# Layer 1 attention in a two-layer decoder: biases folded into the scores and the residual, values of two tokens made ahead of the outputs, weighted products between value moves

## What is computed

```
src = x                                  # (s=4, b=512, f=256): it attends over the FIRST axis, 4 long
qkv = einsum('sbf,pf->sbp', src, in_proj_weight) + in_proj_bias      # p = 3 * 1024
q, k, v = split(qkv, 3)                  # 16 heads of 64
attn = softmax(q / 8 @ k.T)              # 4 x 4 for each b and head
out = attn @ v                           # 4 x 1024 for each b
x = layernorm(x + out @ out_proj_weight.T + out_proj_bias)
```

## Time and profile before

| | |
|---|---|
| median of three runs | 2261.79 us |
| profiled execution, first to last instruction | 2256.1 us |
| busy over the span: PE / DVE / ACT / GpSimd | 89% / 68% / 51% / 42% |
| mean granted TensorE clock | 0.955 of full speed (2.4 GHz) |
| layer 1's attention in the span | from about 527 to 889 us |

### The profile page before, as it was taken

How to read it: one execution, slowest core, us unless ns; L and a number is a source line. 1 busy time by engine, 2 the same in 40 slices (tenths; PEclk the granted TensorE clock), 3 DMA queues, 4 the chain that set the end, 5 groups by cost and what they waited for, 6 DMA issues and landing times. The chain is left out here.

```text
span 2256.1 us, 35858 instructions
## 1 busy us (share of the span) xinstructions
PE 2013.2 (89%) x12740; PEld 1400.3 (62%) x12740; DVE 1528.9 (68%) x2458; ACT 1150.2 (51%) x2210; POOL 950.5 (42%) x738
## 2 busy tenths in 40 slices
PE   7898867997988985899999999999999997699997
PEld 4565547994344444556666666665666664599996
DVE  5777764555888796688788778887787886322223
ACT  3332311111457546678775877677776773233333
POOL 2233232322222131366666756575665665222223
PEclk9999988998999997999999999999999998799998
DMA  4100017211000001000000010000000001621113
GB/s 158 39 23 22 23 48 281 97 67 66 1 0 1 0 30 67 1 1 1 30 1 1 10 30 1 1 10 1 1 1 1 10 1 40 243 109 36 39 36 124
DMA packets 36714, 93.29 MB, mean 41 GB/s; under 512 B 5415, under 2 KB 24379, under 8 KB 31934
## 3 DMA queue, kind: packets, MB, share of 16 engines
q1 hardware_dynamic: 30462, 74.72, 9.2%
q0 software_dynamic: 6080, 16.29, 2.2%
HBM read 76.56 MB, written 14.44 MB: 40 GB/s over the span
## 5 line engine op out<-in xcount | busy, mean ns | idle before, releaser
L2169 POOL TENSOR_TENSOR x_total<-x_total,x_pt 128x1024 f32<-128x1024 f32 x189 | 446.4, 2362 | 172.6 <-ACT x_pt L2255 155.3
L2277 ACT ACTIVATE x_pt<-PS,x_maskf 128x512 f32<-128x512 f32 x544 | 332.1, 689 | 165.8 <-PE PS L2591 164.9
L2376 DVE TENSOR_TENSOR PS<-x_pt,PS 128x512 f32<-128x512 f32 x480 | 333.4, 695 | 65.5 <-ACT x_pt L2277 28.3
L2394 DVE TENSOR_TENSOR x_pt<-x_pt,PS 128x1024 f32<-128x1024 f32 x320 | 320.1, 1050 | 0.7 <-PE PS L2609 0.7
L2591 PE MATMUL PS<-x_qs,x_ks 64*128 64x256 f32 x2176 | 281.3, 395 | 1.5 <-ACT x_pt L2277 1.5
L2568 PE MATMUL PS<-x_pt,x_vs 128*64 128x256 f32 x2108 | 264.2, 390 | 20.5 <-ACT x_pt L2255 10.6
L2255 ACT ACTIVATE x_pt<-x_pt 128x1536 f32<-128x1536 f32 (+1 forms) x160 | 266.5, 1667 | 13.8 <-DVE x_pt L2394 13.8
L1165 PEld LDWEIGHTS PS<-m_xT,m_own 128*128 128x128 f32 x1984 | 235.4, 195 | 8.3 <-DVE m_own L1245 2.9
L1165 PE MATMUL PS<-m_xT,m_own 128*128 128x128 f32 x1984 | 236.3, 278 | 4.1 <-DVE m_own L1245 2.4
L2591 PEld LDWEIGHTS PS<-x_qs,x_ks 64*128 64x128 f32 x2176 | 199.2, 188 | 65.2 <-issue 39.3
L2568 PEld LDWEIGHTS PS<-x_pt,x_vs 128*64 128x64 f32 x2108 | 142.3, 137 | 138.5 <-issue 65.1
(11 more groups left out here) (315 smaller groups left out, 2894.3 us busy)
## 6 DMA issues: line engine op xcount, KB each, us to landing
f_w<-in_L_ffn_w SPq DMA_DIRECT2D x32, 1024.0 KB
a_ctxT<-in_ctxT SPq DMA_DIRECT2D x8, 800.5 KB, 4.4
l_w<-in_ctx SPq DMA_DIRECT2D x4, 1024.0 KB
f_w<-ys SPq DMA_DIRECT2D x16, 256.0 KB, 5.5
l_w<-in_L_attn_w SPq DMA_DIRECT2D x6, 512.0 KB
a_xT<-in_xT SPq DMA_DIRECT2D x4, 512.0 KB, 5.9
X<-in_x SPq DMA_DIRECT2D x1, 2048.0 KB, 10.9
xr<-a_xn SPq DMA_DIRECT2D x16, 128.0 KB, 1.7
```

The source lines that it names most:

```text
L2169: ins = nc.gpsimd.tensor_tensor(total2[:], first, tile[:, 2 * k + 2:2 * k + 4, :], ALU.add)
L2277: nc.scalar.activation(pt[:, s % 2, t, :].rearrange("p (h n) -> p h n", h=2), PS[:, first:first + 2, half], ACT.Identity, bias=maskf[:, b ...
L2376: ins = nc.vector.tensor_tensor(acc, tile, acc, ALU.max)
L2394: nc.vector.tensor_tensor(p_, p_, PS[:, MB, None, :].to_broadcast([P, at.stop - at.start, SPAN]), ALU.subtract).then_inc(lowered, 1)
```

## The change

The bias of a chunk is no longer added on PE. Because a softmax over keys is unchanged by terms that depend on the query alone, and the rest is linear, the query and key biases turn into one term for each query token, head and key token, made from x by a small matmul: per group, use QK (now a use of its own) multiplies the turned x by `wab` (two blocks of 16 columns, folded once from the natural weights and the biases in `fold_biases`), ACT moves it to `ab`, GpSimd makes `both` from it (`bias_terms`), and DVE adds `both` to the scores ahead of the softmax. The value bias passes through the softmax unchanged, so its projection plus the output bias is a vector `vb`, made once, which GpSimd adds to X (`residual_input`) before the residual. `l1_prepare` and the bf16 pieces are gone; new inputs natural (2 MB), across, cols and bo are loaded by SyncE between `yg` and `wo`.

The value chunks of tokens 0 and 1 (uses VF to VF + 3) now come ahead of the outputs on PE and ACT; the outputs, their projections and the exponential are at OUT_AT = VF + 4. At the last three value moves ACT makes one part each of the following group's products (`early`), for groups 1 and 2. The diff, cut to its core:

```diff
-        USES = TURNED + len(CHUNKS)
+        USES = TURNED + len(CHUNKS) + 1
         QK = TURNED + 4 * B
+        VF = QK + 1
+        OUT_AT = VF + 4
+
+        def chunk(u):
+            return CHUNKS[u - TURNED if u < QK else u - TURNED - 1]
...
+            sp.dma_start(natural, g["L1_attn_natural"]).then_inc(natural_loaded, 16)
+            sp.dma_start(across[:].rearrange("p i c h -> p (i c h)"), g["L1_attn_across"]).then_inc(small_loaded, 16)
+            sp.dma_start(bcols[:].rearrange("p i c -> p (i c)"), g["L1_attn_cols"]).then_inc(small_loaded, 16)
+            sp.dma_start(bo[:], g["L1_attn_bo"]).then_inc(small_loaded, 16)
             sp.dma_start(wo[:], g["L1_attn_wo"]).then_inc(wo_loaded, 16)
...
+            def bias_terms(grp):
+
+                pool.wait_ge(fold_ready, 1)
+                pool.wait_ge(ring_free, grp * USES + QK + 1)
+                own = ab[:, grp % 2]
+                nc.gpsimd.tensor_tensor(own[:, :, 0:H1], own[:, :, 0:H1], fold[:, None, KD * AB:].to_broadcast([P, B, H1]), ALU.add)\
+                    .then_inc(ab_raised, 1)
+                pool.wait_ge(ab_raised, grp + 1)
+                if grp >= 1:
+                    pool.wait_ge(sc_ready, grp)
+                nc.gpsimd.tensor_tensor(both[:], own[:, :, None, 0:H1].to_broadcast([P, B, B, H1]),
+                                        own[:, None, :, H1:AB].to_broadcast([P, B, B, H1]), ALU.add).then_inc(both_ready, 1)
+
+            def residual_input(grp):
+
+                pool.wait_ge(vb_ready, 1)
+                pool.wait_ge(ring_done, grp * USES + TURNED)
+                x = X[:].rearrange("p (s j) d -> p s j d", j=J)[:, :, grp, :]
+                nc.gpsimd.tensor_tensor(x, x, vb[:, None, :].to_broadcast([P, B, D]), ALU.add).then_inc(xb_ready, 1)
...
+                bias_terms(grp)
+                residual_input(grp)
...
+                elif u == QK:
+                    if grp >= 2:
+                        act.wait_ge(both_ready, grp - 1)
+                    dst, src = ab[:, grp % 2].rearrange("p s n -> p (s n)"), src[:, 0:B * AB]
...
+                if u == QK:
+                    act.wait_ge(fold_done, 1)
+                    nc.scalar.copy(fold[:], PS[:, PB, 0:KD * AB + H1]).then_inc(fold_ready, 1)
                 move(0, u)
...
+            early = 0
             for grp in range(J - 1):
-                made = 0
+                made, early = early, 0
                 for u in range(USES):
-                    if u == QK:
+                    if u == OUT_AT:
                         for s in range(B):
                             turned(grp, s)
                         exponent(grp + 1)
                     move(grp + 1, u)
                     made = weigh_to(grp, made, min(made + (0 if u < 2 else 3 if u < 6 else 2), 16 if u < 6 else 24 if u < 10 else 32))
+                    if u > VF + 4 and grp + 1 < J - 1:
+                        early = weigh_to(grp + 1, early, early + 1)
...
+                dve.wait_ge(xb_ready, grp + 1)
...
+                if grp == 0:
+                    dve.wait_ge(small_loaded, 48)
+                    dve.wait_ge(vb_done, 1)
+                    nc.vector.tensor_tensor(vb[:], PS[:, PB + 1, 0:D], bo[:], ALU.add).then_inc(vb_ready, 1)
+                dve.wait_ge(both_ready, grp + 1)
+                link(nc.vector.tensor_tensor(now, now, both[:], ALU.add))
...
-                dve.wait_ge(ring_free, grp * USES + QK + 4)
+                dve.wait_ge(ring_free, grp * USES + VF + 4)
...
+                elif u == QK:
+                    if grp == 0:
+                        pe.wait_ge(fold_ready, 1)
+                    for s in range(B):
+                        for k in range(KD):
+                            mm = nc.tensor.matmul(bank[:, s * AB:(s + 1) * AB], xT[:, s, k, :], wab[:, k, :],
+                                                  start=(k == 0), stop=(k == KD - 1))
                 else:
-                    s, m = CHUNKS[u - TURNED]
+                    s, m = chunk(u)
                     if u == TURNED:
                         pe.wait_ge(ring_free, grp * USES + TURNED)
                     at = slice(m * 512, (m + 1) * 512)
-                    nc.tensor.matmul(bank, ones3[:], bias[:, at], start=True, stop=False)
                     for k in range(KD):
-                        mm = nc.tensor.matmul(bank, xT[:, s, k, :], w[:, k, at], start=False, stop=(k == KD - 1))
+                        mm = nc.tensor.matmul(bank, xT[:, s, k, :], w[:, k, at], start=(k == 0), stop=(k == KD - 1))
                 mm.then_inc(ring_done, 1)
+
+            def fold_biases():
+
+                pe.wait_ge(natural_loaded, 16)
+                pe.wait_ge(small_loaded, 48)
+                for i in range(2):
+                    for k in range(KD):
+                        out = PS[:, PB, k * AB + i * H1:k * AB + (i + 1) * H1]
+                        for c in range(KF):
+                            nc.tensor.matmul(out, natural[:, i, c, k * P:(k + 1) * P], across[:, i, c, :],
+                                             start=(c == 0), stop=(c == KF - 1))
+                for c in range(KF):
+                    mm = nc.tensor.matmul(PS[:, PB, KD * AB:KD * AB + H1], bcols[:, 0, c:c + 1].to_broadcast([P, P]),
+                                          across[:, 0, c, :], start=(c == 0), stop=(c == KF - 1))
+                mm.then_inc(fold_done, 1)
+                pe.wait_ge(wo_loaded, 16)
+                for c in range(KF):
+                    mm = nc.tensor.matmul(PS[:, PB + 1, 0:D], bcols[:, 1, c:c + 1].to_broadcast([P, P]), wo[:, c, :],
+                                          start=(c == 0), stop=(c == KF - 1))
+                mm.then_inc(vb_done, 1)
...
-            pe.wait_ge(bias_sent, 16)
-            pe.wait_ge(ones_ready, 1)
-            for u in range(USES):
+            for u in range(QK):
+                fill(0, u)
+            fold_biases()
+            for u in range(QK, USES):
                 fill(0, u)
             for grp in range(J):
                 if grp + 1 < J:
-                    for u in range(QK):
+                    for u in range(OUT_AT):
                         fill(grp + 1, u)
                 turn_out(grp, 0)
                 for s in range(B):
@@ -1895,7 +1947,7 @@
                         turn_out(grp, s + 1)
                     project(grp, s)
                 if grp + 1 < J:
-                    for u in range(QK, USES):
+                    for u in range(OUT_AT, USES):
                         fill(grp + 1, u)
...
```

More of the change, by code:

```diff
@@ L1109, in multiply @@
         y_done, y_ready = sem("y_done"), sem("y_ready")
-        pace, prepared = sem("pace"), sem("prepared")
+        pace = sem("pace")
         block = ctx.enter_context(nc.Block(no_gpsimd_drain=True))
@@ L1142, in _ @@
                     scatter(i - 1)
-                if layer == 0:
-                    g["l1_prepare"](pool, prepared, i - 6)
             for q in range(YN):
@@ L1458, in layer1_attention @@
         RING, PB, OB = 4, 4, 6
-        bias, bias_sent = g["l1_bias"], g["l1_bias_sent"]
         gates = g["gates0"]
@@ L1462, in layer1_attention @@
         y_added, y_counted, y_stats, y_rs, y_normal = sem("y_added"), sem("y_counted"), sem("y_stats"), sem("y_rs"), sem("y_normal")
-        ones3 = sb("ones3", [3, P], BF16)
-        ones_ready = sem("ones_ready")
+        across = sb("across", [P, 2, KF, H1])
+        bcols = sb("bcols", [P, 2, KF])
+        bo = sb("bo", [P, D])
+        AB = 2 * H1
+        fold = sb("fold", [P, KD * AB + H1])
+        wab = fold[:, 0:KD * AB].rearrange("p (k n) -> p k n", k=KD)
+        vb = sb("vb", [P, D])
+        ab = sb("ab", [P, 2, B, AB])
+        both = sb("both", [P, B, B, H1])
+        small_loaded, natural_loaded = sem("small_loaded"), sem("natural_loaded")
+        fold_done, fold_ready, vb_done, vb_ready = sem("fold_done"), sem("fold_ready"), sem("vb_done"), sem("vb_ready")
+        ab_raised, both_ready, xb_ready = sem("ab_raised"), sem("both_ready"), sem("xb_ready")
         xT = sb("xT", [P, B, KD, P])
@@ L1485, in layer1_attention @@
         o = sb("o", [P, B, P1])
+        natural = o[:].rearrange("p s n -> p (s n)").rearrange("p (i c d) -> p i c d", i=2, c=KF)
         oT = sb("oT", [P, 2, KF, P])
@@ L2698, in one_more, with attention_biases @@
     return np.concatenate([c, np.zeros((1,) + c.shape[1:], c.dtype)], 0)
+def attention_biases(w, b, out):
+    of_query, of_key, of_value = (b[i * P1:(i + 1) * P1] for i in range(3))
+    across = np.zeros((P, 2, KF, H1), b.dtype)
+    for i, one in enumerate((of_key, of_query)):
+        for c in range(KF):
+            for h in range(P // HD1):
+                rows = slice(h * HD1, (h + 1) * HD1)
+                across[rows, i, c, c * (P // HD1) + h] = one[c * P:(c + 1) * P][rows]
+    return {
+        "L1_attn_natural": w[:2 * P1].reshape(2, KF, P, D).transpose(2, 0, 1, 3),
+        "L1_attn_across": across.reshape(P, 2 * KF * H1),
```

(5 more changed lines are left out.)

45 lines of the change are left out of this document (9 added, 36 removed).

## The result

| | before | after |
|---|---|---|
| median | 2261.79 us (7 runs) | 2269.94 us (7 runs) |
| profiled execution: its own time | 2257.38 us | 2264.38 us |
| its span | 2256.1 us | 2262.3 us |
| mean granted clock over the span | 0.955 | 0.951 |

The ratio of after to before is 1.0031, with a 95% interval of 1.0021 to 1.0041. A second comparison, beside other kernels, gave 1.003 (1.0021 to 1.004). The change costs about 8 us, or 0.3%: little, but both intervals lie above 1. The forecast was 2266.6 with 2256 to 2276.

What follows compares the result with a forecast made beforehand. ACT and DVE were taken to bound each cycle, PE only through value waits and group 0. Shifts of +0.5, plus 4.3 for the clock in the fold, gave +4.8 on 2261.79: 2266.6 us, range 2256 to 2276.

Steps and rivals of the forecast that it cites:

- group 0, to D0: Stage start to DVE's first addition of group 0's weighted products: +0.1 from new PE work, +4.3 from half clock.
- cycle 0: From DVE's first weighted-product addition in group 0 to group 1's: value wait -5.56, added DVE work and lock stall +1.56.
- cycle 1: Between those first additions in groups 1 and 2: early weighted products +3.1, added DVE work +1.56, value wait -2.3.
- last group: End of the stage: ACT weighs right after the softmax instead of behind eight value moves, -0.3.
- Value waits: DVE's waits for the first two tokens' values vanish because four chunks move ahead of the turning: 5.56, 2.3 and 2.3.
- 0.52 us go per chunk, that is hidden: PE's chunks without bias records: 12.5 us saved per group, 50 in all, expected to gain nothing.
- DVE's added work: After the scores: new addition 0.46 us plus 1.1 us stall against GpSimd, in groups 1, 2 and 3.
- Early parts: Three next-group parts between value moves delay DVE's pair 4 to 27.6 us after its first addition: +3.1 in two cycles.
- the clock did fall: Rival for the fold: PE keeps 2.4 GHz, the rest goes as forecast, 2262.3 us; 22%.
- PE was not the bound of the cycle: Rival: PE sets the cycle, which falls from 81.8 to 69.8 us, giving 2226 in all; 7%.
- the early parts were not free: Rival: early weighted products cost nothing, so 6.2 us come back, 2260.4 with the clock's fall, 2256.1 without; 13%.
- the 14.0 of all at half clock: Rival: all new group 0 PE work runs at half clock, costing 14.0 us more, 2276.3; 18%.

Runs made afterwards that it cites:

- e4: Changed kernel with folded biases alone: value chunks all behind the outputs again, no early weighted products; 2254.56 us, ratio 0.9979.
- e1: Changed kernel without the early weighted products of the next group between the last value moves; 2254.13 us, ratio 0.9973.
- e6: Kernel before the change with only the first two tokens' value chunks made and moved ahead of the turned outputs; 2244.99 us, ratio 0.9927.
- e7: e1 with group 0's exponent between its value moves, four group 0 parts among its last moves, parts and moves reordered by table; 2240.77 us, ratio 0.9908.
- e11: Changed kernel, early parts kept, with the rewritten table of parts due behind each move in groups 1 and 2; 2254.14 us, ratio 0.9966.
- e9: Kernel before the change, bias records kept, with values ahead, group 0's exponent between value moves and the rewritten order; 2250.3 us, ratio 0.9953.
- e10: e7 with two parts of group 0 instead of four ahead of the turned inputs' moves, its table matched; 2235.8 us, ratio 0.9887.
- e12: e10 with vb's 256-column matmuls in pairs among the fold's narrow ones, and GpSimd's residual input moved as in e8; 2237.29 us, ratio 0.9892.
- e3: Changed kernel with one of eight partial products in each fold, 10 records instead of 80, biases incomplete; 2253.62 us, ratio 0.9965.
- e2: Changed kernel with group 0's exponential directly behind the third value chunk's move, ahead of the last five moves; 2262.57 us, ratio 1.0002.
- e8: e1 with GpSimd's 128x1024 residual input put behind the same group's first output, in the next group's score loop; 2256.21 us, ratio 0.9981.

## Why the prediction was right

The predicted and the measured shift of each step, in the profiled executions. The measured ones are differences of the table above to two digits.

| step | forecast | measured |
|---|---|---|
| group 0, to D0 | +0.1 and +4.3 by the clock | +5.9 |
| cycle 0 | -5.56 + 1.56 = -4.0 | -4.4 |
| cycle 1 | +3.1 + 1.56 - 2.3 = +2.4 | +2.1 |
| cycle 2 | +3.1 + 1.56 - 2.3 = +2.4 | +2.0 |
| last group | -0.3 | -0.4 |
| stage | +4.8 | +5.1 |
| before and behind the stage | 0 | -0.8 and +1.9 |

The span grew by 6.2 us, the medians by 8.15. The sum held because its steps held, within 1.5 us each; in one of them, the early parts, two errors cancelled, and that was luck:

- *Group 0.* Fold, `vb` and score terms took 19.0 us (566.21 to 585.24); 14.0 + 4.3 = 18.3 were forecast. The clock fell in the fold and recovered in `vb`, as taken. The slack of 1.1 us between ACT's last move and the exponent is used up: the move at 599.25 is followed by the exponent at 599.73. The other 0.8 us of the difference are not resolved. No row before the change showed a clock's fall like this one; the 4.3 us was a choice between bounds, and the pitches give some 5.0.
- *Value waits.* Gone in all groups, and DVE goes straight from the softmax into the product, as forecast. The attribution was wrong. The fold's shorter chunks remove 8.1 of these 10.2 us by themselves (e4), and "0.52 us go per chunk, that is hidden" is the step that failed: before, PE's chunks were on the path through the value waits. The sum didn't feel it, as the changed kernel has both parts and the wait goes once.
- *DVE's added work.* The addition took 0.93 us to the next start (669.38 to 670.31) where 0.46 + 1.1 was forecast, and the product before it 0.13 more: 1.06 for 1.56. GpSimd in after, at the end of group 1's scores:

```profile
666.09 1.60 POOL L1546 TENSOR_TENSOR l_both<-l_ab 128x256 f32<-128x256 f32 x1
667.64 2.35 POOL L1554 TENSOR_TENSOR X<-X,l_vb 128x1024 f32<-128x1024 f32 x1
```

The large addition started 1.7 us ahead of DVE's, so that only its tail was in the way.
- *Early parts.* Pair 4 stands 27.7 us behind D, forecast 27.6. But the 3.1 us that the forecast took off came from the cycle before the change, 24.46. Without the early parts it is 22.95 (e1), so they cost 4.76 each. The sum was saved by 1.5 us that this place gains and that I had not counted. The shorter chunks are enough for that gain: e4, without any value made ahead, has 22.95 in both cycles, while e6, values ahead alone, has 24.2 in cycle 1 and 22.9 in cycle 2. Before the change DVE's second addition waits for ACT's parts in cycle 1, and in e1 and e4 it doesn't:

```profile
694.37 1.23 DVE L1765 TENSOR_TENSOR l_o<-l_o,l_wp 128x1024 f32<-128x1024 f32 x1 [1.70 <-ACT l_wp L1604]
```

- *Early parts, their cover.* The forecast's reason, that ACT is short of DVE's release and not of time, is what e1, e7 and e11 show.

The miss of 3.3 us against the median is 0.3 in the stage, 1.1 around it, and 1.9 between the profiled executions and the medians. The median lies above 2268.6, the line from which the forecast called a time slower; to that side it had given 30%, to "same" 58%. The rivals: the clock did fall; PE was not the bound of the cycle, but its chunks paced ACT in e9; the early parts were not free; and the fall cost some 5 us, not the 14.0 of all at half clock.

The changed kernel gives away two gains. The early parts cost it 9.7 us of stage (15 by the medians, e1). The order left as it was, that of the parts and of group 0's exponent, costs another 17.5 (18 by the medians, e10 against e1).

## What to carry to other kernels

Work moved into an engine's idle time gains nothing if that idle time stands in front of a wait; look at what the engine does right after the release, and move out of that stretch what someone else waits for. Two edits that remove the same wait don't add: run each alone and both. After an edit that changes a duration, write the order of the work anew before judging the edit: the same fold cost 6.6 us of stage under one order and gained 13.5 under another (10.2 of them where nothing else differed).

## What the runs showed of the hardware

- The granted clock fell from 1.00 to 0.50 while PE ran 16-column matmuls back to back without a gap: 5.2 us after the first in after, 4.7 in e10. Their pitch went from 0.11 to 0.21 us, that of 256-column records from 0.215 to 0.43. With a fifth of the records 256 columns wide the fall came after 11.7 us (e12), and with ten narrow records instead of 80 it didn't come in the fold at all (e3).
- The half-clock stretch in the fold was 10.2 us long in some kernels (after, e1, e4) and 13.7 in others (e2, e7, e8, e10, e11) with the same instructions on PE up to there, worth 1.4 us at D0 between e1 and e8. So a difference of 1 to 2 us between two kernels can be the clock's alone.
- GpSimd's addition of 128x256 took 0.72 us in group 0 of after and 1.60 beside a DVE product; DVE's of the same size took 0.42 us in e8 and 0.90 beside GpSimd's large addition in after. With the 128x1024 products of both, DVE's took 3.47 instead of 1.22.
